# A Mamba and mixture-of-experts kernel: routing read from PSUM, a shorter B and C path, and a reordered head and tail

## The reference

```python
x = x + mamba(ctx, layernorm(x))        # ctx [4,256,128], z = layernorm(x) [4,256,256]
x = x + moe(layernorm(x))
# mamba: uc = silu(conv4(in_proj(ctx)) + b); dt, Bm, Cm = x_proj(uc)
#   delta = softplus(dt_proj(dt) + dt_b);  A = -exp(A_log)          (256 channels, 16 states)
#   state = state * exp(delta * A) + delta * uc * Bm;  y = sum_n state * Cm
#   out = (y + D * uc) * silu(z)
# moe: p = softmax(x @ Wg); top 2 of 8 experts; capacity 320 rows an expert, in token order,
#   what is over is dropped;  out = sum_k gate_k * relu(x @ w1[e]) @ w2[e]   (256 -> 1024 -> 256)
```

## Time and profile before

| | us |
|---|---|
| runs | 350.09, 352.02, 355.56 (median 352.02) |
| profiled execution | 351.8 |
| its span, first to last instruction | 350.0 |
| busy PE / VectorE / GpSimd / ScalarE | 257.1 / 247.2 / 214.4 / 167.3 |
| mean granted TensorE clock | 0.816 |
| first scan, last scan, start of expert 0's matmuls | 22.86, 180.11, 211.61 |

### The profile page before, as it was taken

The page is one execution under the profiler, slowest core; times in us unless marked ns, Lnnn a source line. Parts: engine busy times, 40 slices in busy tenths (PEclk is TensorE's granted clock), DMA queues, the critical chain, the costliest instruction groups (busy, mean ns, idle before and its releaser), DMA issues. The chain is left out here.

```text
span 350.0 us, 4871 instructions
## 1 busy us (share of the span) xinstructions
PE 257.1 (73%) x1508; PEld 232.2 (66%) x1508; DVE 247.2 (71%) x397; ACT 167.3 (48%) x355; POOL 214.4 (61%) x168
## 2 busy tenths in 40 slices
PE   8756264875708828356653599999999999999970
PEld 7535154754607627245652498899999999999970
DVE  1498986999997898999995055466567585857610
ACT  1479424775424944255314026364747465463710
POOL 0494745985960779726915018548677777768642
PEclk9696856898657885656756569999999999999996
DMA  7754410007000083001105205635554545464110
GB/s 169 228 167 137 196 48 0 0 2 267 6 0 0 32 301 98 24 0 47 45 0 176 74 1 180 220 121 170 216 187 149 186 148 189 154 243 166 80 50 34
DMA packets 14641, 39.45 MB, mean 113 GB/s; under 512 B 2794, under 2 KB 9628, under 8 KB 11712
## 3 DMA queue, kind: packets, MB, share of 16 engines
q1 hardware_dynamic: 11360, 32.23, 27.4%
q0 software_dynamic: 2816, 6.32, 4.9%
q10 hardware_dynamic: 448, 0.70, 0.8%
HBM read 31.81 MB, written 8.47 MB: 115 GB/s over the span
## 5 line engine op out<-in xcount | busy, mean ns | idle before, releaser
L328 POOL TENSOR_TENSOR dbu<-du,bsb 128x1024 f32<-128x1024 f32 x31 | 72.4, 2354 | 11.2 <-DVE h L1109 5.4
L1109 DVE TENSOR_TENSOR_SCAN h<-ps,dbu 128x1024 f32<-128x1024 f32 x32 | 73.1, 2284 | 3.6 <-ACT ps L504 3.3
L504 ACT ACTIVATE ps<-delta,anegs 128x255 f32<-128x255 f32 x128 | 53.0, 462 | 34.8 <-DVE h L1109 31.0
L700 PE MATMUL ps<-stack,sels 96*128 96x256 bf16 x80 | 19.3, 338 | 67.6 <-DVE hc L1120 64.9
L700 PEld LDWEIGHTS ps<-stack,sels 96*128 96x128 bf16 x80 | 6.7, 109 | 75.7 <-issue 71.2
L1270 DVE SCALAR_TENSOR_TENSOR htlo<-ps,hthi 128x320 fp32r<-128x320 f32 x64 | 30.5, 487 | 35.6 <-ACT hthi L624 21.3
L730 PE MATMUL ps<-cst,hc 128*128 128x128 f32 x256 | 48.5, 352 | 2.1 <-DVE hc L1120 2.1
L730 PEld LDWEIGHTS ps<-cst,hc 128*128 128x128 f32 x256 | 43.4, 189 | 3.6 <-DVE hc L1120 2.3
L404 POOL TENSOR_TENSOR w2lo<-w2raw,w2hi 128x512 fp32r<-128x512 f32 x30 | 38.3, 1300 | 10.9 <-ACT w2hi L615 10.7
L895 PE MATMUL ps<-xthi,w1hi 128*128 (+1 forms) x128 | 40.1, 313 | 0.4 <-issue 0.4
L895 PE MATMUL ps<-hthi,w2hi 128*128 128x320 f32 x128 | 40.3, 315 | 0.0
(11 more groups left out here) (143 smaller groups left out, 501.6 us busy)
## 6 DMA issues: line engine op xcount, KB each, us to landing
w1raw<-in_w SPq DMA_DIRECT2D x8, 1024.0 KB
w2raw<-in_w SPq DMA_DIRECT2D x8, 1024.0 KB
bsb<-b_rows SPq DMA_DIRECT2D x6, 1024.0 KB, 6.0
expert_rows<-fill SPq DMA_DIRECT2D x1, 2580.0 KB, 10.5
xe<-expert_rows SPq DMA_DIRECT2D x8, 258.0 KB
out<-x SPq DMA_DIRECT2D x4, 256.0 KB, 5.2
sels<-in_sel SPq DMA_DIRECT2D x1, 768.0 KB, 10.8
xnat<-in_x SPq DMA_DIRECT2D x1, 768.0 KB, 11.4
```

The costliest lines, as they stand in the source:

```text
L328: nc.gpsimd.tensor_tensor(dbu[j % DRING][:], du[:, :, None, cols(b)].to_broadcast([P, EC, 2, L]), bsb[b % 2][:, None, 2 * p:2 * p + 2, :]. ...
L504: ins = nc.scalar.activation(decays(g % SLOTS_DA)[:, c, i * L + 1:(i + 1) * L], delta[:, c, b * L + 1:(b + 1) * L], ACT.Exp, scale=anegs[: ...
L1109: nc.vector.tensor_tensor_scan(h[g % HRING][:].rearrange("p c n t -> p (c n t)"), decays(g % SLOTS_DA).rearrange("p b t -> p (b t)"), dbu[ ...
```

## The change

- B and C are split in two fp32r parts instead of three bf16 parts (`stack` and `sels` have 64 partitions, one column of `sels` is read with a step of 0 for all 128 weight columns). `parts` becomes `lo_rows`, one instruction. `sels` is loaded as 8 KB to `brow` and converted by ScalarE as its first instruction.
- B of batch 0: only pairs 0 and 1 come by PE (`CASTS = 2`); the other six come by DRAM (`spread_b(0)`), ahead of the filling of the rows in DRAM.
- Routing: `choose` and `place` read logits and counts in PSUM; the copies on ScalarE (`logits_out`, `counts_out`), `topf`, `multi` and two of `etop` go. The exponential takes bias `ntop` and scale `rx`. `counts` starts from the base of each expert (a float32 matmul of one partition) and counts each of the two choices, so that the sum is the slot number.
- Order: x_proj and dt_part at p = 1 in each batch, softplus at p = 3, `place` and `counts` a step earlier, in the last batch all of the routing one or two steps earlier; `send(b - 1)` at p = 7 of batch b on GpSimd instead of p = 1 of the next. Head: five warming matmuls, then seven later; dt_part ahead of x_proj. Tail: the turn of x1 and the logits are ahead of `place_rows`; four and four warming matmuls in place of eight and eight; `low_w1` of expert 0 ahead of `choose`.

```diff
@@ constants @@
-XPC = 3 * BC
+XPC = 2 * BC
+CASTS = 2
...
@@ SyncE @@
-            sp.dma_start(sels[:], sel).then_inc(s["sel_in"], 16)
+            sp.dma_start(brow[0:XPC, 0:BC], sel).then_inc(s["sel_in"], 16)
...
-            sp.wait_ge(s["fill_made"], 1)
-            sp.wait_ge(s["delta_done"], EC)
-            sp.dma_start(xe_dram.rearrange("(t p) r -> p t r", p=P),
-                         fill[:, None, :].to_broadcast([P, SLOTS // P, ROW])).then_inc(s["xe_filled"], 16)
...
+            spread_b(0)
+            sp.wait_ge(s["fill_made"], 1)
+            sp.dma_start(xe_dram.rearrange("(t p) r -> p t r", p=P),
+                         fill[:, None, :].to_broadcast([P, SLOTS // P, ROW])).then_inc(s["xe_filled"], 16)
             spread_b(1)
@@ GpSimd, drive and the loop @@
-                if b == 0:
+                if j < CASTS:
                     pool.wait_ge(s["b_done"], j + 1)
                 else:
-                    pool.wait_ge(s["b_lo_in" if p < PAIRS // 2 else "b_hi_in"], 16 * b)
+                    pool.wait_ge(s["b_lo_in" if p < PAIRS // 2 else "b_hi_in"], 16 * (b + 1))
...
-                    if p == 4:
-                        softplus_d(1)
-                        softplus(1)
-                        delta_u(1)
+                if b >= 0 and b + 1 < B and p == 3:
+                    softplus_d(b + 1)
+                    softplus(b + 1)
+                    delta_u(b + 1)
...
-                    if p == 1 and b >= 2:
-                        if b == 2:
+                    if p == 7:
+                        if b == 1:
                             pool.wait_ge(s["xe_filled"], 16)
-                        send(b - 2)
+                        send(b - 1)
                 drive(j)
@@ ScalarE @@
+                for j in range(b * BT, (b + 1) * BT):
+                    ins = nc.scalar.activation(etop[:, j, :], top[:, j, :], ACT.Exp, bias=ntop[:, j:j + 1],
+                                               scale=rx[:, j:j + 1])
...
+            act.wait_ge(s["sel_in"], 16)
+            nc.scalar.activation(sels[:], brow[0:XPC, 0:BC], ACT.Copy).then_inc(s["sel_done"], 1)
             act.wait_ge(s["wdt_psum"], 1)
@@ TensorE @@
+                    ins = nc.tensor.matmul(ps[:, bank, i * L:(i + 1) * L], sels[:, n:n + 1].to_broadcast([XPC, P]),
                                            stack[:, cols(b)], start=(i == 0), stop=True, skip_group_check=True)
...
-            keep_clock(11, V0BANK)
+            keep_clock(5, V0BANK)
...
+            keep_clock(7, BBANK)
+            pe.wait_ge(s["wdt_done"], 1)
+            for k in range(EC):
+                pe.wait_ge(s["u_done"], k + 1)
+                ins = dt_part(0, k, V0BANK)
+            ins.then_inc(s["v_psum"], 1)
...
+            pe.wait_ge(s["slots_done"], B - 1)
             pe.wait_ge(s["scan_done"], SLOTS_DA + STEPS)
+            keep_clock(4, DABANK)
+            turn_x1(B - 1)
+            keep_clock(4, DABANK)
+            logits(B - 1)
             pe.wait_ge(s["xe_in"], 32)
             place_rows(0)
-            pe.wait_ge(s["pos_done"], B - 1)
-            turn_x1(B - 1)
+            counts(B - 1)
             place_rows(1)
-            logits(B - 1)
-            keep_clock(8, CBANK)
-            counts(B - 1)
-            keep_clock(8, CBANK)
@@ VectorE @@
-            def parts(b, bank):
+            def lo_rows(b):
...
-                link(nc.vector.tensor_tensor(rest[:], ps[0:XPC, bank, 0:L], stack[:, bs], ALU.subtract))
-                nc.vector.tensor_copy(stack[BC:2 * BC, bs], rest[BC:2 * BC, :])
-                link(nc.vector.tensor_copy(stack[2 * BC:3 * BC, bs], rest[2 * BC:3 * BC, :]))
-                nc.vector.tensor_tensor(stack[2 * BC:3 * BC, bs], rest[2 * BC:3 * BC, :],
-                                        stack[2 * BC:3 * BC, bs], ALU.subtract
+                dve.wait_ge(s["brow_done"], b + 1)
+                nc.vector.tensor_tensor(stack[BC:2 * BC, cols(b)], ps[BC:2 * BC, BBANK, 0:L],
+                                        stack[BC:2 * BC, cols(b)].bitcast(F32), ALU.subtract
                                         ).then_inc(s["stack_done"], 1)
...
             variance(last, row_stats(last))
+            for m in range(WP):
+                low_w1(0, m)
             choose(last)
             place(last)
```

More of the change, by code:

```diff
@@ L120, in build @@
         topi = sb("topi", [P, TILES, NE], U32)
-        topf = sb("topf", [P, TILES, TOPK])
         rsum = sb("rsum", [P, TILES])
-        oh = sb("oh", [P, TILES, TOPK, NE])
+        oh = sb("oh", [P, TILES, TOPK, NE], BF16)
         ohc = sb("ohc", [P, TILES, TOPK, NE])
-        cum = sb("cum", [P, BT, NE])
-        multi = sb("multi", [P, TILES, NE], BF16)
-        pos = sb("pos", [P, TILES, TOPK])
+        over = sb("over", [P, BT, NE])
+        place_of = sb("place_of", [P, BT, NE])
+        ntop = sb("ntop", [P, TILES])
         slot = sb("slot", [P, TILES, TOPK])
@@ L154, in build @@
         du = sm("du", [P, EC, T])
[L155 to L158 removed]
+        sels = sm("sels", [XPC, BC], F32R)
+        stack = sm("stack", [XPC, T], F32R)
+        brow = sm("brow", [XPC, L])
         xnt = sm("xnt", [P, KC, BT * P])
@@ L1080, in _ @@
             softplus_t(0, V0BANK)
+            lo_rows(0)
             dve.wait_ge(s["sp_d"], 1)
@@ L1180, in place @@
                 tiles = tiles_of(b)
+                dve.wait_ge(s["pos_psum"], b + 1)
+                at = ps[:, BBANK, 0:BT * NE].rearrange("p (t e) -> p t e", e=NE)
+                link(nc.vector.tensor_tensor(over[:], at, cst[:, CEND:CEND + BT * NE].rearrange("p (t e) -> p t e", e=NE),
+                                             ALU.is_ge))
+                link(nc.vector.scalar_tensor_tensor(out=place_of[:], in0=over[:], scalar=DROPPED, in1=at,
+                                                    op0=ALU.mult, op1=ALU.add))
+                link(nc.vector.tensor_tensor(ohc[:, tiles, :, :], oh[:, tiles, :, :],
+                                             place_of[:, :, None, :].to_broadcast([P, BT, TOPK, NE]), ALU.mult))
+                link(nc.vector.tensor_reduce(slot[:, tiles, :], ohc[:, tiles, :, :], AX.X, ALU.add))
                 dve.wait_ge(s["top_exp"], b + 1)
+                nc.vector.tensor_copy(sloti[:, tiles, :], slot[:, tiles, :]).then_inc(s["slots_done"], 1)
                 link(nc.vector.tensor_reduce(rsum[:, tiles], etop[:, tiles, :], AX.X, ALU.add))
@@ L1314, in _ @@
                                         ).then_inc(s["takes_done"], 1)
-            for m in range(WP):
-                low_w1(0, m)
             for c in range(KC):
@@ L1353 @@
     consts[:, CIOTA:CIOTA + NE] = np.arange(NE)
-    sel = np.zeros((3, BC, BC, P), ml_dtypes.bfloat16)
-    for n in range(BC):
-        sel[:, n, n, :] = 1.0
+    consts[:, CBASE:CEND] = np.tile(CAP * np.arange(NE), BT)
+    consts[:, CEND:NCONST] = np.tile(CAP * np.arange(1, NE + 1), BT)
     arrays = {
```

237 lines of the change are left out of this document (87 added, 150 removed).

## The result

The changed kernel takes 326.14 us (median of 4 runs, 321.98 to 326.88) against 351.64 us of the kernel before (350.09 to 355.56): ratio 0.925, 95% interval 0.913 to 0.937. It is faster, and inside the range of 306 to 331; the forecast of 317 lies 9 us too low. The profiled execution took 325.75 us, with a span of 323.9 (350.0 before).

The account below looks back on a forecast made before the run. VectorE was taken to bound the scans, with the experts untouched, so time won ahead of them shortens the kernel. 351.8 - 4 (head) - 21.5 (scans) - 9.2 (tail) = 317 us; range 306 to 331.

Parts of the forecast that it names:

- The head: Up to the first scan: earlier PE start and dt parts running alone, -4 us (0 to -5).
- Parts: Scans, batches 1 to 3: three instructions with a PSUM input at 0.42 us replace 10.4 us of VectorE work, -9.1 us.
- Choose: Scans, routing on VectorE: six instructions become three, so fewer gaps between GpSimd products are waited for, -5.5 us.
- Waits: Scans: VectorE no longer waits for batch 1's softplus, ScalarE's copies of logits and counts, or the exponential, -9.0 us.
- New wait before scan 7: Batch 0: power, softplus and du stand ahead of GpSimd's product 7, so scan 7 waits, +3.2 us.
- Place, sends, B over DRAM: Place loses one instruction three times, -0.5 us; sends covered by 3 us; batch 0's B over DRAM costed at nothing.
- The tail: Last VectorE product to expert 0's first matmul: `sloti` after 11.6 us instead of 20.8, -9.2 us (-6 to -11).
- The first: Rival: in place, two or three instructions wait 2.35 us in two batches, +9 to +14, 328 us; chance 0.28 shared by three rivals.
- the fourth: Rival: products 7, 19, 27 stall the scans and batch 0's B is late, 329 us; chance 0.28 shared by three rivals.
- the third: Rival: nothing is shut out in choose and the clock rises early in the tail, -8 to -9, 308 us; chance 0.15.
- The fifth: Rival: fp32r casts make PE the bound at 5.5 us a step, slower than before, 361 us; chance 0.02.
- the second: Rival: `sels` and `cwb` land late (+4), one product a batch is late (+6), 327 us; chance 0.28 shared by three rivals.

Follow-up runs that it names:

- h_nmz: Changed kernel with batch 0's `nmz` moved from behind VectorE's first product of B to right behind the difference of the rows; 323.4 us, no ratio.
- x_sbuf: Changed kernel plus one unused VectorE subtraction of 32 x 256 elements, both inputs in SBUF, in batches 1 to 3; 326.71 us, ratio 0.923.
- gap2: Changed kernel plus two unused copies of the `nmx` instruction at the end of choose in batches 0 to 2; 325.9 us, ratio 0.925.
- c_bf16: Changed kernel with the rows of B and C and the selecting columns as bf16 in place of fp32r; 323.15 us, ratio 0.916.
- z_late: Changed kernel with the power of z's variance on GpSimd moved from ahead of product 7 to ahead of product 9; 319.53 us, ratio 0.907.
- t_warm: Changed kernel plus four warming matmuls behind expert 0's first turn and six behind the last counts, in the tail; 323.47 us, ratio 0.918.

## Why the prediction was right, and where its sizes were off

Against the forecast the head came out 4.7 us long, the scans 4.6 us long and the tail 0.9 us short. The range held because it was wide enough for both misses.

- **The bound and the balance** were right: VectorE in the scans, the experts untouched (138.4 to 138.6 us), so what was won ahead of them is what the kernel won.
- **The head: -4 foreseen, +0.7 came.** In parts: to the end of `u` -0.6 (foreseen -1), from there to the softplus -1.0 (foreseen -3), from the softplus to the first scan +2.3 (foreseen +0.4). "It will run the dt parts alone ... so 2.3 to 4.0 us go" left out the seven warming matmuls that the change puts ahead of them: the dt parts took 2.16 us, but started 2.0 us after `u`. The half speed was allowed for too narrowly, with 0.6 us on the first product: PE started it at 3.9 as foreseen, took 2.08 us for 1.12, and in the profiled execution went on at half speed up to about 13 us. Where it reached full speed before 7 us, the first scan came at 20.19 to 20.75, inside "18.3 to 20.9". The largest part is an omission: `nmz` now stands beside a product of GpSimd, 2.3 us, and `h_nmz` gives 1.6 to 1.9 of them back. `u` did wait for `sels`, as feared, and `cwb` landed in time (GpSimd starts on it at 9.23).
- **Parts: -9.1 foreseen, -9.0 came** (from 10.3 us in the scans to 1.3). The reason I gave ("that form doesn't wait") is true of the kernel before (0.42 us inside a row of products), but isn't needed here: the change's three instructions stand where GpSimd is idle, and `x_sbuf` shows that an SBUF form takes 0.41 us there too. What went is mostly the casts: the six in the scans took 7.8 us, where six of 0.28 would be 1.7.
- **Choose: -5.5 foreseen, -7.3 came** (15.9 us of `topf` to `nmx` in the scans, now 8.6). The instructions were 1.53, 2.35 and 0.15 in both batches, for the 0.4, 2.3 and 2.3 foreseen. The mechanism, one short instruction per gap and sometimes a second, stands in `gap2`. What I took for fixed is a toss: in the nine executions up to `c_bf16`, `nmx` took 2.37 us 6 times of 18. That it was short in both batches of the profile after is luck.
- **Waits: -9.0 foreseen, -5.6 came** (all of VectorE's idle time fell by 2.3 us, with 3.3 of the new wait in it). In the scans this is the term that was mis-sized. The softplus of batch 1 and ScalarE's copies are waited for no longer, but reading PSUM directly moves the wait to PE: 1.04, 1.04 and 0.50 us for the logits. ScalarE holds scans 3, 11 and 19 for 0.57, 1.37 and 2.10 where it was 0.93, 0.76 and 1.59, and the last product waits 1.16 us for its cast, which it had not done.
- **Not foreseen: `vx`**, +2.3 us: it takes 2.46 us in batch 3, where the change moves the variance a step ahead and into GpSimd's products (the one of 146.7 to 149.1), and took 0.17 there before.
- **New wait before scan 7: +3.2 foreseen, 3.31 came.** `z_late` shows that its cause is the power in front of softplus, and that it could be had for nothing.
- **Place, sends, B over DRAM: as foreseen.** Nothing in place is above 0.19 us, no scan waits for product 19 or 27, and no scan of batch 0 for B.
- **The tail: -9.2 foreseen, -10.1 came**, from two errors of opposite sign: `sloti` 2.5 us sooner, the way from there 1.5 us longer. The clock that the forecast set at zero, with 2.5 us "at the worst", came at about its worst: `t_warm` gives 1.5 us ahead of the first matmul and 1.1 behind it.
- **The rivals.** The first (exclusion in place) and the fourth (the change doesn't do what it says) are refuted by the rows of place and of product 19; the third did not come in choose, and of its tail the early half came (granted clock 1.00 from 171.0 to 178.0, before it fell). The fifth (PE as the bound) is refuted too: the casts' records are 0.47 us for two at full speed and 0.76 to 0.79 at half. Of the second its first half came, a lost head, for the most part by other causes than the two I named; the one late product, 7, was in the forecast.
- **The signs.** Five came: the second scan 2.2 us after the first, 4.65 us between scans 3 and 4, scan 5 right after the variance, the stall before scan 7, nothing above 0.25 in place. The first scan (23.60 for 18.3 to 20.9), the three lengths in choose and the 9.1 us to `sloti` (for 11 to 13) did not, and of the signs of being wrong one came: `u` behind `sels`.

## What to carry to other kernels

Where VectorE and GpSimd share a stage, the place of a short instruction with two SBUF inputs decides its price, 0.15 or 2.3 us: list for each of them what GpSimd runs at that moment, those that a change only shifts included. Put nothing short that waits for another engine at the head of a queue that feeds the bound. Replacing a copy by a direct read removes the copier's wait only if the producer is early enough: ask what then comes last. And a profile of one execution can hold a head 3 us off: before an edit is credited with a difference, look whether the rows ahead of it agree.
